# A fused cross-attention and LoRA feed-forward layer: more raw buffers, a shifted attention plan, a first chunk of x through a second buffer, and a start with two head halves side by side

## The reference

```
h = layernorm(x)                                 # no scale, no shift
q = rope(h @ Wq)      32 heads of 128            # Wq 1024 x 4096
k = rope(ctx @ Wk)     8 heads of 128            # Wk 1024 x 1024
v = ctx @ Wv           8 heads of 128            # Wv 1024 x 1024
logits = 30 * tanh(q k^T * 0.0884 / 30)          # 128 x 128 per sequence and head
weights = softmax(where(mask, logits, -1e30))
x = x + (weights @ v) @ Wo                       # Wo 4096 x 1024
h = layernorm(x)
base = h @ W_base.T + b_base                     # 1024 x 1024
w = softmax of the 2 largest of h @ W_router.T   # 8 experts
lora = 2 * sum_e w_e * (h @ A_e.T) @ B_e.T       # rank 16
out = x + base + lora
```

## Time and profile before

| | |
|---|---|
| median of 3 runs | 2158.23 us |
| the profiled execution | 2158.16 us, span 2156.4 us |
| granted TensorE clock, mean | 0.997 |
| busy: TensorE, VectorE, ScalarE, GpSimd | 99%, 78%, 41%, 14% |
| moved by DMA | 508.50 MB, mean 236 GB/s |

### The profile page before, as it was taken

How to read it: one execution, slowest core, us unless ns; L and a number is a source line. 1 busy time by engine, 2 the same in 40 slices (tenths; PEclk the granted TensorE clock), 3 DMA queues, 4 the chain that set the end, 5 groups by cost and what they waited for, 6 DMA issues and landing times.

```text
span 2156.4 us, 26390 instructions
## 1 busy us (share of the span) xinstructions
PE 2132.3 (99%) x9429; PEld 1729.3 (80%) x9429; DVE 1674.3 (78%) x2571; ACT 883.1 (41%) x1342; POOL 294.0 (14%) x359
## 2 busy tenths in 40 slices
PE   9999999999999999998999999999999999999999
PEld 7888888888888888876777877777787777888887
DVE  6976888888886666676877779997999879857443
ACT  3323243222241111155565556655666556423221
POOL 0350001111131000012101111111112111100000
PEclk9999999999999999999999999999999999999999
DMA  8698697665596665698666885689767965696741
GB/s 327 234 332 290 218 334 271 231 221 211 209 339 229 211 212 201 221 279 263 189 193 196 233 224 174 202 273 276 194 195 221 298 182 163 210 368 265 294 184 66
DMA packets 207987, 508.50 MB, mean 236 GB/s; under 512 B 20720, under 2 KB 54128, under 8 KB 205808
## 3 DMA queue, kind: packets, MB, share of 16 engines
q1 hardware_dynamic: 187376, 443.31, 62.7%
q0 software_dynamic: 20480, 63.50, 9.3%
HBM read 357.26 MB, written 149.16 MB: 235 GB/s over the span
## 4 chain that ended last, share of the span: by engine, by line
PE 87%; DMA 7%; DVE 3%; ACT 1%; issue 1%; SPq 0%; POOL 0%; DVEq 0%; ACTq 0%
PE ps L377 28%; PE ps L378 28%; PE ps L379 28%; DMA RB<-rD 3%; DMA rD<-r 2%; PE ps L920 1%; DMA X2D<-stg 1%; DMA raw<-gran 1%; DVE Y L990 1%; DMA Y<-xT 1%; DVE Rl L330 1%; DVE ps L330 0%; DVE ps L905 0%; DVE Pl L330 0%; DMA kraw<-ctxT 0%
## 5 line engine op out<-in xcount | busy, mean ns | idle before, releaser
L377 PE MATMUL ps<-Ah,Rh 128*128 128x512 f32 x1024 | 400.9, 391 | 4.2 <-DVE Y L990 4.2
L378 PE MATMUL ps<-Al,Rh 128*128 128x512 f32 x1024 | 399.9, 391 | 0.0
L379 PE MATMUL ps<-Ah,Rl 128*128 128x512 f32 x1024 | 399.5, 390 | 0.0
L379 PE MATMUL ps<-Xq,qW 128*128 128x512 f32 x896 | 348.6, 389 | 0.0
L377 PE MATMUL ps<-Xq,qW 128*128 128x512 f32 x896 | 348.5, 389 | 0.0
L378 PE MATMUL ps<-Xq,qW 128*128 128x512 f32 x896 | 348.5, 389 | 0.0
L330 DVE TENSOR_TENSOR Rl<-raw,Rh 128x1024 fp32r<-128x1024 f32 x174 | 212.2, 1220 | 57.6 <-ACT Rh L326 57.2
L326 ACT ACTIVATE Rh<-raw 128x1024 fp32r<-128x1024 f32 x176 | 185.5, 1055 | 154.6 <-PE ps L379 127.1
L377 PEld LDWEIGHTS ps<-Ah,Rh 128*128 128x128 f32 x1024 | 193.2, 189 | 46.8 <-DVE Y L990 4.6
L379 PEld LDWEIGHTS ps<-Ah,Rl 128*128 128x128 f32 x1024 | 193.1, 189 | 40.8
L378 PEld LDWEIGHTS ps<-Al,Rh 128*128 128x128 f32 x1024 | 193.2, 189 | 40.5
(11 more groups left out here) (217 smaller groups left out, 3881.7 us busy)
## 6 DMA issues: line engine op xcount, KB each, us to landing
raw<-gran SPq DMA_DIRECT2D x177, 512.0 KB, 5.6
QSD<-qW SPq DMA_DIRECT2D x64, 512.0 KB, 3.1
qD<-qt SPq DMA_DIRECT2D x128, 256.0 KB, 3.3
qW<-QSD SPq DMA_DIRECT2D x64, 512.0 KB, 3.7
qf<-qD SPq DMA_DIRECT2D x64, 512.0 KB, 8.5
RB<-rD POOLq DMA_DIRECT2D x128, 256.0 KB, 6.8
qraw<-gran SPq DMA_DIRECT2D x48, 512.0 KB, 4.3
kD<-kst SPq DMA_DIRECT2D x32, 512.0 KB, 3.8
```

The lines of the kernel that those rows point to most:

```text
L377: put("pe", waits, lambda e: e.matmul(pe_out, lh, rh, start=first, stop=False, skip_group_check=more))
L378: put("pe", [], lambda e: e.matmul(pe_out, lh, rl, start=False, stop=False, skip_group_check=more))
L379: return put("pe", [], lambda e: e.matmul(pe_out, ll, rh, start=False, stop=last, skip_group_check=more), mark)
```

## The change

- `OW` gets four more raw buffers (at 40, 44, 56 and 60 KB, where the sixth and seventh factors of the query products lie, and later the second half of Ah and Al). They serve for the twelve splits of V's last chunk; from the first of the last four V jobs on, three raw buffers are in use again, and Ah and Al of odd groups wait for the four.
- In the attention plan z becomes 8 gi - 22, with the sums at z+8, the rows at z+12, the values at z+14 and on: scores and sums come one place earlier, rows and values stay. Between sums and the first value are six places, not five. Scores and values now fall in the same (even) places. Group 1's values go from 2, 3, 5, 6 to 1, 2, 4, 5.
- For the first chunk x is loaded into Y2. The first group's output jobs are copied from the bank into Y by ScalarE, and Y2 is added to it from SBUF by whichever engine is free.
- The first two K granules are both loaded in halves, ahead of the other context parts, and the first two K jobs go side by side: for each of the eight feature blocks three matmuls for the one and three for the other.
- The load of `cs` waits until the last context part of the first chunk has been rounded.

```diff
+        more = [here(f"more{i}", [P, 1024], F32, 40 + 4 * i + 8 * (i // 2)) for i in range(4)]
...
-        d_c = dma(cs[:, :], cst, [], "d_cst", 196)
...
+        def k_both():
+            got = [bank() for _ in k_first]
+            for k in range(KC):
+                for w, (b, waits) in enumerate(got):
+                    lh, ll = KW.tiles(w, k)
+                    m = three(ps[b][:, :], lh, ll, cX[0][:, k, :], cX[1][:, k, :], k == 0, k == KC - 1,
+                              (KW.marks[w] + waits if k == 0 else late[w] if k == 4 else []) + buf_marks["X"][k],
+                              cn("pe_job") if k == KC - 1 else None)
+                    got[w] = b, m if k == KC - 1 else waits
+            last_job[0] = m
+            return got
...
-        k_first = [0]
-        KW.marks[0], first_late = KW.split2(gran[GK], kRh[0][:, :], kRl[0][:, :])
-        KW.n = 1
-        KW.free[0] = None
+        k_first, late = [0, 1], {}
+        for w in k_first:
+            KW.marks[w], late[w] = KW.split2(gran[GK + w], kRh[w][:, :], kRl[w][:, :])
+            KW.free[w] = None
+        KW.n = 2
         ctx_load(0, "X", KW, [1, 2, 3])
-        k_first.append(KW.granule(gran[GK + 1]))
         ctx_load(1, "A", KW)
         gate = buf_marks["A"][-1]
+        d_c = dma(cs[:, :], cst, buf_marks["X"][-1][0:1], "d_cst", 196)
...
+                    if cp + j + i == 0:
+                        first, second = k_both()
+                        pending.append(lambda first=first, second=second: k_evac(0, 0, [first])(second))
+                        continue
...
-        OW.raw_free = [s_done + late_q for _ in raw]
+        OW.raw_free = [s_done + late_q for _ in raw] + [x_free[5], x_free[5], x_free[6], x_free[6]]
+        OW.raws = raw + more
...
+                if (c, g) == (0, 0):
+                    a = put("act", [m] + y_free[n // 2], lambda e: e.activation(y, ps[b][:, :], ACT.Copy), cn("act_o"))
+                    bank_free[b] = [a]
+                    y_acc[c, n] = [tt("flex", y, y, Y2[:, n, :], ALU.add, [a, y_marks[c, n // 2]], "y")]
+                    y2_free.append(y_acc[c, n][0])
+                    return
...
+                if b4 == 0:
+                    a_war[1] = a_war[1] + sum(OW.raw_free[RAW:], [])
+                    OW.raws, OW.raw_free = raw, OW.raw_free[0:RAW]
...
-                 1: ((-11, -9, -7, -6), -4, -2, (2, 3, 5, 6)),
+                 1: ((-11, -9, -7, -6), -4, -2, (1, 2, 4, 5)),
...
-            z = 8 * gi - 21
-            scores, sums, rows, values = first.get(gi, (range(z, z + 8, 2), z + 8, z + 11, range(z + 13, z + 21, 2)))
+            z = 8 * gi - 22
+            scores, sums, rows, values = first.get(gi, (range(z, z + 8, 2), z + 8, z + 12, range(z + 14, z + 22, 2)))
...
-                        y_load(0, j)
+                        y_marks[0, j] = dma(Y2[:, 2 * j:2 * j + 2, :], xT[0][:, 2 * j:2 * j + 2, :], y2_free, f"d_y{j}", 512)
```

More of the change, by code:

```diff
@@ L468, in job @@
                     m = three(ps[b][:, :], lh, ll, bh[:, k, :], bl[:, k, :], k == 0, k == KC - 1,
-                              (KW.marks[w] + waits if k == 0 else first_late if k == 4 and w == 0 else []) + buf_marks[buf][k],
+                              (KW.marks[w] + waits if k == 0 else []) + buf_marks[buf][k],
                               cn("pe_job") if k == KC - 1 else None)
```

## The result

The changed kernel takes 2169.68 us (median of 8 runs, 2161.66 to 2178.47), the kernel before beside it 2153.01 us (8 runs, 2146.58 to 2160.96). The ratio is 1.0072, with a 95% interval of [1.0052, 1.0093]: slower by 0.7%, where 2147 us and a gain had been forecast. The profiled execution took 2164.22 us, 5.5 under its median, with a span of 2162.3 us and a mean granted clock of 0.995. The prediction took the profiled execution of before (2158.16 us) for a typical one, going by three runs; the eight runs put it 5 us above the median. The traces therefore show 6 us of the difference and not all of it. One execution in what follows, of the kernel of number 8, took 2586.57 us at a mean granted clock of 0.771, and its ratio is formed without it.

The account below looks back on a forecast made before the run. TensorE was taken as the bound, busy 2132.3 of 2156.4 us, leaving its standstills and slow clock after them to win. From 2158.2 us, -7 (places), -3 (x), 0 (raw buffers) and -1.1 (start) gave 2147 us, range 2136 to 2163.

Parts of the forecast that it names:

- the six places: Attention plan: scores and sums one place earlier shorten the sums' waits at chunk ends; -7 us, between -11.5 and +3.6.
- The pile: Chunk ends: 3.2 us of queueing on VectorE, 2.0 before the sums' copy and 1.2 before the reciprocal, would go.
- the signs at the end of the prediction: Chunk ends, if right: sums' waits below 1 us each, and the sums' copy starting 1.2 us after its matmuls.
- the upper bound: Chunk ends: -11.5 us, from 8.2 us of shorter sums' waits and 3.3 us from no more half-rate clock stretches.
- this group's sums, the chain and 3.3 us: Attention: the next sums need this group's sums, its reciprocal chain of transfers, and 3.3 us from multiply to exponent.
- the lower bound: Chunk ends: a 1.2 us weight split comes between VectorE's multiply and mask, three times; +3.6 us.
- the sign that the prediction itself gave as a warning: Quiet groups: holes there, which no step expected, would show the prediction wrong.
- x of the first chunk: First chunk's output: the 4.2 us Y wait goes, a short sums' wait comes near 1012; -3 us, bounds 0 and -5.9.
- Raw buffers: V's last chunk: the wait hangs on a query store, not on raw buffers; 0 us, between -6.3 and +9.8.
- rival (c): V's last chunk: splits arrive late, and loads pulled forward delay query store and first chain; slower, 2167 us, chance 0.12.
- Start: First 48 matmuls: end near 23.2 us instead of 24.4; -1.1 us, bounds -2.4 and +1.5.
- (a): Chunk ends: the order holds, places give 0 and waits stay 2.7 to 3.0 us; 2155 us, chance 0.25.

Follow-up runs that it names:

- number 8: The kernel before with only the products moved one place later, the RB row loads left in place: 2144.71 us, 0.9952.
- number 2: The kernel before with the change's new attention places alone (scores and sums one place earlier): 2185.12 us, 1.0128.
- 3: The changed kernel with the layer norm's X2D stores issued from SyncE's queue instead of GpSimd's: 2164.51 us, 1.0048 of the kernel before.
- 5: The changed kernel with the second layer norm begun one place earlier: 2159.22 us, 1.002 of the kernel before.
- 6: The changed kernel with the second layer norm begun one place later: 2170.28 us, 1.0082 of the kernel before.
- 1: The changed kernel with the attention plan of before, its other parts kept: 2151.69 us, 0.9994 of the kernel before.
- 4: The kernel before with the layer norm's X2D stores issued from SyncE's queue instead of GpSimd's: 2158.85 us, 1.0012.
- 10: The kernel before with the seven raw buffers alone: 2155.9 us, 1.0.
- number 11: The kernel before with the new start alone (two K jobs side by side, constants later): 2154.4 us, 0.9996.
- number 12: The kernel before with only x of the first chunk loaded through Y2: 2152.19 us, 0.9993.
- 7: The kernel before with rows and the first three of a group's four products one place later, scores and sums unmoved: 2144.56 us, 0.994.
- 9: The whole change, but with rows and products moved back instead of scores and sums forward: 2144.6 us, 0.9961 of the kernel before.

## Why the prediction was wrong

**The step that failed is the term of the six places: -7 us, with bounds of -11.5 and +3.6, where the plan cost 17 us within the change and 28 alone.** Two things in it were wrong.

- *What the moved steps meet.* The term priced the chain at the chunk ends and put every other place at nothing ("In quiet groups nothing is due"), because in a repeating plan only distances were counted. Distances inside the plan repeat, but the layer norm in the background, the next chunk's x and the stores don't move with it. The working asked what stands behind VectorE's multiply and never what stands ahead of the moved scores on the queues of ScalarE and VectorE. At 1434 and 1676 these are a rounding and a low part that wait for the norm's stores. Such waits were in the trace of before (19.0 us in 12 waits; none of the rows showed them), where no sums waited behind them. The timeline at 1439 shows this for 8.7 us of waits, and number 2 has the same two for 10.4. That they make up the whole loss isn't shown: an earlier norm removes them and gives back about 11 us, a later one breaks them up and gives back nothing.
- *The pile.* "So less work is piled up behind when the next chain starts" is the sentence that the -7 stands on. Its first half came true in the trace of the change: VectorE's waits for RB fell by 17.8 us, and the copy of the sums starts 1.2 us after its matmuls at all three chunk ends, as the signs at the end of the prediction ask. The pile didn't go; it moved to the reciprocal. That is 3.1, 2.4 and 2.7 us late in the change (before 1.2, 1.2 and 3.8), so copy and reciprocal together are 8.2 us late instead of 8.7. In the four other kernels with the sums forward (numbers 2, 3, 5 and 6) the reciprocal is 2.4 to 6.6 us late; in those with the plan of before (the kernel before and numbers 1, 4 and 10 to 12) 0.7 to 4.6, with products moved back (numbers 7 to 9) 0.0 to 1.7. The ranges overlap at the third chunk end, not at the first two (2.4 to 6.6 against 1.1 to 2.3). Why it is later isn't settled: the written order on VectorE and the loads of x that it waits for change together, and no run took them apart.

Behind both lies that moving the product back and moving scores and sums forward were taken for one, since both make the distance six places. The runs separate them: -10 us one way (0.9952), +28 the other (1.0128). That the bounds hold the first is luck, for they were worked out for the second. And the 3.3 us of clock in the upper bound rest on a wait of 2.2 us that brought no slow stretch; in number 8 a wait of 2.2 us at 977 was followed by 3.4 us at the lower clock level (0.50).

**What held.** That the next group's sums are bound by this group's sums, the chain and 3.3 us: from the multiply on it is 3.1 us in number 2 and 3.1 in the change (1499.13 to 1502.24). The pile of 3.2 us in the earlier trace rows was the right thing to look at: in number 8 it vanishes at the chunk end they show, and with it every wait for an exponent, the -11.5 of the upper bound nearly to the full. The mask behind a weight split, which the lower bound was made of, is there, but takes the place of other work and lengthens nothing. And the sign that the prediction itself gave as a warning, holes where no step expects any, is what came; they had been looked for in quiet groups, and they came before the chunk ends.

**x of the first chunk, -3.** The mechanism is right: the 4.2 us wait is gone, and a short wait of the sums came (1.8 us in number 12; 1.53 at 1011.01 in the change, forecast 1.5 near 1012). Measured -1.5 us with an interval of -4.7 to +1.7, which holds both -3 and nothing.

**Raw buffers, 0.** Right: 1.0 [0.9984, 1.0017]. The reason given was right as well. The wait of ScalarE for the stored query, 5.65 us in the earlier trace rows, became 8.00 us in the change, as "more loads ahead of that store make it later" says, and TensorE waits 4.0 us there instead of 2.4 and 2.2. The late fourth split of rival (c) didn't occur: a wait of 0.3 us at 937.4 and one of 0.7 at 943.8 are all.

**Start, -1.1.** The two traces seem to bear it out. The first 48 matmuls (the row of the last, before and after)

```profile
24.17 0.39 PE L379 MATMUL ps<-Xh,kRl 128*128 128x512 f32 x1
```
```profile
21.79 0.39 PE L379 MATMUL ps<-Xh,kRl 128*128 128x512 f32 x1
```

end 2.4 us earlier, and at the next wait that both have, for the low part of a K weight (at 149.21 before, at 147.27 after), 1.9 of it is left. But that is luck of the one trace of before. The same row in number 12, which has the old start, and in number 11, which has the new one:

```profile
20.62 0.39 PE L379 MATMUL ps<-Xh,kRl 128*128 128x512 f32 x1
```
```profile
21.53 0.39 PE L378 MATMUL ps<-Xh,kRl 128*128 128x512 f32 x1
```

Over all traces the matmul starts between 19.95 and 24.17 us with the old start (seven traces, median 20.70) and between 21.37 and 22.21 with the new one (seven, median 21.79); the wait near 147 comes at 145.0 to 149.2 and at 146.7 to 147.7. So the new start is steadier and by the medians about 1 us slower, and the -1.1 was worked out against the slowest of seven. In the time of whole runs neither can be seen (0.9996, an interval of 7 us).

**The rivals.** None described what happened. (c) had the right sign and, by luck, nearly the time (2167 us), for a cause that didn't occur. (a) describes the second chunk end, where the wait stays, but not the first, where it is gone. None moved the plan against the background work.

## What to carry to other kernels

A distance between two steps can be widened from either end, and in this kernel the ends weren't alike: moving the consumer back only lets it wait less, moving the producer forward also puts it, and all that it queues for, against whatever runs there. Before a step is moved, list for each in-order engine what stands just ahead of its new place, at the places where background work runs and not only in a quiet stretch. And where one trace and the medians differ by several us, attribute with the trace and size with the runs; a term of 1 us needs more than one trace of the kernel before.

## What was not expected of the hardware

Transfers of 256 and 512 KB issued between 1423 and 1426 took 10 to 11 us to land, on either queue; over the whole run the median of the RB loads is 6.1 us. Moving these stores to the other queue made the small copies of the chain no shorter: 8.3, 8.8 and a load of 9.4 us one after the other at the second chunk's end, against 7.7, 7.2 and 8.8 before the move. That fits copies whose time goes by what else is in flight, on whichever queue, but no run here varied the traffic alone.
